# Second layer of a two-layer kernel: scores and the G product as three passes over split operands

## The reference, cut to what matters

```python
x = x + 0.5 * ffn0(layernorm(x))
x = x + attn0(layernorm(x))
x = x + 0.5 * ffn0(layernorm(x))
x = x + 0.5 * experts(layernorm(x))
x = x + attn1(layernorm(x))           # the part that is changed
x = x + 0.5 * experts(layernorm(x))

def attn1(x, Wk, Wq, Wv, Wa, Wb):
    k, q, v = x @ Wk.T, x @ Wq.T, x @ Wv.T
    e = einsum("biq,bjq->bij", q, k @ Wa.T)
    return softmax(e) @ (v @ Wb.T)
```

## Time and profile before

| | us |
|---|---|
| median of 3 runs | 1031.23 (1031.03 to 1032.40) |
| profiled execution, span from first to last instruction | 1028.6 |
| around the span, by the median | 2.6 |
| PE busy in the span | 946.0 (92%) |
| DVE busy | 734.3 (71%) |
| ACT busy | 556.6 (54%) |
| GpSimd busy | 618.5 (60%) |

### The profile page before, as it was taken

The page is one execution under the profiler, slowest core; times in us unless marked ns, Lnnn a source line. Parts: engine busy times, 40 slices in busy tenths (PEclk is TensorE's granted clock), DMA queues, the critical chain, the costliest instruction groups (busy, mean ns, idle before and its releaser), DMA issues. The chain is left out here.

```text
span 1028.6 us, 16112 instructions
## 1 busy us (share of the span) xinstructions
PE 946.0 (92%) x4589; PEld 701.4 (68%) x4589; DVE 734.3 (71%) x2076; ACT 556.6 (54%) x1189; POOL 618.5 (60%) x579
## 2 busy tenths in 40 slices
PE   3999999999999999999999998899988999889994
PEld 2777777777766767767777775488764666658773
DVE  5778789898989889999999976344433667634442
ACT  4554665675857758566555442245425777525441
POOL 4677778777667677676787785434441245433443
PEclk9999999999999999999999999999999999999998
DMA  6880000000000000000000002156524000016561
GB/s 172 354 363 1 1 1 1 1 1 1 1 1 1 1 1 1 1 1 1 11 9 4 11 11 85 54 164 194 174 70 137 1 23 22 22 56 194 174 181 33
DMA packets 42904, 65.17 MB, mean 63 GB/s; under 512 B 7153, under 2 KB 25121, under 8 KB 40640
## 3 DMA queue, kind: packets, MB, share of 16 engines
q1 hardware_dynamic: 37824, 55.59, 16.7%
q0 software_dynamic: 4992, 8.54, 2.6%
HBM read 37.20 MB, written 28.74 MB: 64 GB/s over the span
## 5 line engine op out<-in xcount | busy, mean ns | idle before, releaser
L379 PE MATMUL bank<-split 128*128 128x512 f32 x544 | 245.4, 451 | 9.5 <-DVE ud L1341 3.7
L381 PE MATMUL bank<-split 128*128 128x512 f32 x544 | 216.0, 397 | 0.0
L380 PE MATMUL bank<-split 128*128 128x512 f32 x544 | 214.6, 394 | 0.0
L894 ACT ACTIVATE sil<-bank 128x512 f32<-128x512 f32 x128 | 76.0, 595 | 147.7 <-PE bank L381 147.2
L379 PEld LDWEIGHTS bank<-split 128*128 128x128 f32 x544 | 103.9, 191 | 41.4 <-issue 10.0
L1287 DVE TENSOR_TENSOR act<-act,wT 128x512 f32<-128x512 f32 x128 | 123.1, 962 | 4.4
L380 PEld LDWEIGHTS bank<-split 128*128 128x128 f32 x544 | 104.2, 191 | 26.5 <-issue 10.5
L381 PEld LDWEIGHTS bank<-split 128*128 128x128 f32 x544 | 103.4, 190 | 24.0
L1283 DVE TENSOR_TENSOR act<-bank,sil 128x512 f32<-128x512 f32 x128 | 88.0, 687 | 43.5 <-issue 22.4
L1717 POOL TENSOR_TENSOR act<-act 128x512 f32<-128x512 f32 x64 | 86.6, 1353 | 29.4 <-DVE act L1287 29.2
L1723 POOL TENSOR_TENSOR split<-act,split 128x512 fp32r<-128x512 f32 x64 | 92.5, 1447 | 18.1 <-ACT split L963 17.9
(11 more groups left out here) (294 smaller groups left out, 2011.5 us busy)
## 6 DMA issues: line engine op xcount, KB each, us to landing
e<-e_dram SPq DMA_DIRECT2D x92, 256.0 KB, 3.1
rows_in<-yw SPq DMA_DIRECT2D x17, 1056.0 KB, 18.0
xin<-rows_in SPq DMA_DIRECT2D x46, 132.0 KB, 3.1
x<-rows_out SPq DMA_DIRECT2D x8, 256.0 KB, 5.1
rows_in<-yw,slot_i POOLq DMA_INDIRECT x64, 2.3
rows_out<-ob,ids POOLq DMA_INDIRECT x46, 2.3
out<-ob,ids POOLq DMA_INDIRECT x46, 2.5
act<-b_dram SPq DMA_DIRECT2D x2, 256.0 KB, 3.5
```

The lines of the kernel that those rows point to most:

```text
L379: mm(dst, w[0], m[0], start=start, stop=False, **more)
L380: mm(dst, w[0], m[1], start=False, stop=False, **more)
L381: return mm(dst, w[1], m[0], start=False, stop=stop, **more)
L894: af(sil[(k - 1) % 2][:, :], bank[BH1[STEPS[k - 1][0] % 2]][:, :], ACT.Silu).then_inc(silu_done.sem, 1)
```

## The change

y^T, z^T and G are each kept as two fp32r tiles: a high part, which is the rounded value, and a low part, which is what rounding left off. score and y_G become `mm3` of them. The full-precision yT stays for y_U. zT's fp32 copy is gone; ACT writes the high part in its place. ACT writes y twice (high part, then fp32). DVE makes the low parts of y and z by subtraction (`y_low`, `z_low`), at two new places of its list, and the low part of G once, before the first experts. New waits: TensorE waits for the low parts before score, y_G and y_U, and for G's low part before the first experts; y_low waits for both of ACT's copies of y, z_low for ACT's copy of z. The new tile `yz` holds the parts of y and z.

```diff
-        zT, pr_, pT = mT1, act0[0:2], act0[2:4]
+        pr_, pT = act0[0:2], act0[2:4]
...
+        yz = sb("yz", [P, 8 * S], F32R)
+        yTs = [(yz[:, 4 * i * S:(4 * i + 1) * S], yz[:, (4 * i + 1) * S:(4 * i + 2) * S]) for i in range(2)]
+        zTs = [(yz[:, (4 * i + 2) * S:(4 * i + 3) * S], yz[:, (4 * i + 3) * S:(4 * i + 4) * S]) for i in range(2)]
...
-            sem("yT_saved"), sem("zT_ready"), sem("zT_saved"), sem("v1_ready"), sem("v1_saved"))
+            sem("yT_saved", 2), sem("zT_ready"), sem("zT_saved"), sem("v1_ready"), sem("v1_saved"))
+        yz_low = sem("yz_low", 2)
...
                     pe.wait_ge(*exp_done(main, n - 1))
-                    mm(bank[n % 2][:, :], zT[p][:, rows(n)], yT[p][:, :], start=True, stop=True).then_inc(sc_ready.sem, 1)
+                    pe.wait_ge(*yz_low(main))
+                    mm3(bank[n % 2][:, :], tuple(z_[:, rows(n)] for z_ in zTs[p]), yTs[p], True, True).then_inc(sc_ready.sem, 1)
...
                     pe.wait_ge(*yT_saved(pre))
-                    mm(bank[7][:, :], gmat[:, :], yT[pre % 2][:, :], start=True, stop=True).then_inc(zT_ready.sem, 1)
+                    pe.wait_ge(*yz_low(pre, 1))
+                    mm3(bank[7][:, :], gmats, yTs[pre % 2], True, True).then_inc(zT_ready.sem, 1)
...
                     pe.wait_ge(*zT_saved(pre))
+                    pe.wait_ge(*yz_low(pre))
...
             keep_busy(9)
+            pe.wait_ge(prod_saved.sem, 5)
             tiles(0, 4, expert)
...
-                af(gmat[:, :], bank[2][:, 0:P], ACT.Copy).then_inc(prod_saved.sem, 1)
+                af(gmats[0], bank[2][:, 0:P], ACT.Copy).then_inc(prod_saved.sem, 1)
...
                     act.wait_ge(*ao_ready(pre - 2))
+                    af(yTs[pre % 2][0], bank[7][:, :], ACT.Copy).then_inc(yT_saved.sem, 1)
                     af(yT[pre % 2][:, :], bank[7][:, :], ACT.Copy).then_inc(yT_saved.sem, 1)
...
-                    af(zT[pre % 2][:, :], bank[7][:, :], ACT.Copy).then_inc(zT_saved.sem, 1)
+                    af(zTs[pre % 2][0], bank[7][:, :], ACT.Copy).then_inc(zT_saved.sem, 1)
...
+                def y_low():
...
+                    dve.wait_ge(*yT_saved(pre))
+                    dve.wait_ge(*sc_ready(pre - 2))
+                    v.tensor_tensor(yTs[pre % 2][1], yT[pre % 2][:, :], yTs[pre % 2][0].bitcast(F32), ALU.subtract).then_inc(yz_low.sem, 1)
...
+                def z_low():
...
+                    dve.wait_ge(*zT_saved(pre))
+                    v.tensor_tensor(zTs[pre % 2][1], bank[7][:, :], zTs[pre % 2][0].bitcast(F32), ALU.subtract).then_inc(yz_low.sem, 1)
...
                 maximum(0)
+                y_low()
                 r_stats(r_st, ao_done, -NCH)
                 r_factors(srt)
                 maximum(1)
...
                 r_read(srt, 6)
+                z_low()
                 r_top1(srt)
                 add(0)
                 maximum(3)
...
             dve.wait_ge(prod_saved.sem, 4)
+            v.tensor_tensor(gmats[1], bank[2][:, 0:P], gmats[0].bitcast(F32), ALU.subtract).then_inc(prod_saved.sem, 1)
             tiles(0, 4, expert)
```

More of the change, by code:

```diff
@@ L187, in build @@
         waT = sb("waT", [P, P]); wbT = sb("wbT", [P, P])
-        wak = sb("wak", [P, P]); gmat = sb("gmat", [P, P]); wuT = sb("wuT", [P, P])
+        wak = sb("wak", [P, P]); gmat = sb("gmat", [P, 2 * P], F32R); gmats = gmat[:, 0:P], gmat[:, P:2 * P]; wuT = sb("wuT", [P, P])
         cnt = sb("cnt", [P, E]); cnt_i = sb("cnt_i", [P, E], I32); nt_i = sb("nt_i", [P, E], I32); ntf = sb("ntf", [P, E])
@@ L1648, in y_stats @@
                     aggregate(st, stats_l, part_l, mv_l[st % 2], -0.5, bn_l, stat_l, [(sc_l[st % 2][:, 0, :], *PLAIN)])
+                def y_low():
+                    if pre is None:
+                        return
+                    dve.wait_ge(*yT_saved(pre))
+                    dve.wait_ge(*sc_ready(pre - 2))
+                    v.tensor_tensor(yTs[pre % 2][1], yT[pre % 2][:, :], yTs[pre % 2][0].bitcast(F32), ALU.subtract).then_inc(yz_low.sem, 1)
+                def z_low():
+                    if pre is None:
+                        return
+                    dve.wait_ge(*zT_saved(pre))
+                    v.tensor_tensor(zTs[pre % 2][1], bank[7][:, :], zTs[pre % 2][0].bitcast(F32), ALU.subtract).then_inc(yz_low.sem, 1)
                 maximum(0)
+                y_low()
                 r_stats(r_st, ao_done, -NCH)
```

## The result

The changed kernel takes 1069.24 us (median of four runs, 1066.01 to 1072.36) beside 1031.13 for the kernel before in the same comparison: a ratio of 1.038, 95% interval 1.036 to 1.040. The forecast was 1075, its range 1059 to 1086. The profiled execution took 1067.51, its span 1065.8, against 1028.6 before; the second layer is 40.05 us longer and the rest of the program 2.85 shorter.

The account below looks back on a forecast made before the run. TensorE bounds the second layer now, but the added DVE waits would make DVE's chain late. Span 1028.6 + waits 32.0 + clock falls 11.5 + 2.6 outside the span gave 1075 us, 4.2% slower, range 1059 to 1086.

Parts of the forecast that it names:

- The walk: Second layer's full slot, operation by operation: waits for y_low and z_low lengthen it from 14.15 to 18.78 us, +4.63.
- the fall: TensorE's clock drops in the new pause of about 4 us: 1.6 us a slot, seven slots, 11.5 in all.
- The sum: Whole kernel: profiled span 1028.6 + waits 32.0 + clock 11.5 + 2.6 around the span, 1074.7 us.
- chunk 0's fall: Chunk 0's slot, counted among seven with the new TensorE pause: a clock drop costing 1.6 us.
- The products: score and y_G on TensorE: a split product takes 0.79 us against 0.86, giving back 0.35 us a slot.
- gmat's low part: Before the first experts: making it and TensorE's wait cost nothing, as DVE is idle for 6.42 us there.
- Rival 1: Second layer: waits cost what was forecast, but the clock stays up; 1063 us, chance 22%.
- Rival 2: Second layer: clock falls twice a slot, also in the second pause; another 7 x 1.6, 1086 us, chance 10%.
- Rival 3: Second layer: DVE's waits end before TensorE needs maximum(1), so it stays TensorE-bound; 1024 to 1028 us, chance 3%.

Follow-up runs that it names:

- e1: Changed kernel with y_low moved behind share_of(1) and z_low behind share_of(2) in DVE's list; 1030.69 us, ratio 1.0008 to the kernel before.
- e2: Changed kernel with y_low alone moved later in DVE's list, behind share_of(1); 1047.66 us, ratio 1.017 to the kernel before.
- e3: Changed kernel with z_low alone moved later in DVE's list, behind share_of(2); 1061.44 us, ratio 1.032 to the kernel before.
- e7: Changed kernel with 17 unread products before the second transpose, 2 ahead of r_rank and 6 behind it; 1064.47 us, ratio 1.033 to the kernel before.
- e6: Changed kernel with its copies, subtractions and waits, but score and y_G as single fp32 products; 1073.28 us, ratio 1.041 to the kernel before.
- e8: e1's order, with y_stats first on DVE and unread products (8 and 6) in the slot that only prepares chunk 0; 1028.97 us, ratio 0.9996 to before.
- e9: e8 plus unread products in chunk 0's slot, seven ahead of y_T and four ahead of the first transpose of weights; 1026.51 us, ratio 0.9964 to before.
- e5: Changed kernel without making the low parts of y and z, or waiting for them, from the third chunk on; 1034.49 us, ratio 1.006 to before.
- e4: Changed kernel with 17 unread bf16 products on TensorE ahead of the second transpose of weights; 1068.64 us, ratio 1.038 to the kernel before.

## Why the prediction was right, step by step

**The walk held.** It put maximum(1) at 7.09 us into a full slot (measured 7.02), the second transpose at 8.64 (8.57). From there the clock is low: y_G at 10.13 came at 11.04, z_low at 11.77 at 13.33, maximum(3) at 13.73 at 15.27. The 1.54 us between forecast and measurement at maximum(3) is the fall, which I had put at 1.6 and on exactly this stretch: transpose and mix(0) took 2.47 in place of 1.49, y_G and the hand-over 1.67 in place of 1.00. From maximum(3) to the end of the slot it is 4.95, against 5.05. DVE's idle time ahead of z_low is 4.54 us where I had said 2.5; about 1.6 of it is the fall. e1, e2 and e3 show the mechanism itself, not only its times: move the subtractions behind work that is ready and the loss is gone, move one and a part of it is.

**What the clock is worth** was asked of e7: 1.75 us a full slot, within the 0 to 2.45 that the prediction allowed. So the waits at full clock are 4.32, where the walk had 4.63. That my 1.6 came so close is partly luck. It stood for 3.2 us of work at half speed, as in the first layer; here the clock is low for over 5 us of work, and what counts is the part on the chain: transpose, mix(0), y_G and the hand-over, 4.14 us in place of 2.49. The Trainium skill, "TensorE: Matmul & The Clock Gate", section "Loop structure matters more than you think", shows a long wait (for a DMA, in its example) between matmuls sending the clock down; the trace agrees for a wait on an exponential: 3.69 us of pause, then 0.50.

**The sum came out high.** By the slots, in the order of the prediction (with 1.6 for a fall; seven of them are 11.2, not the 11.5 that stands there):

| | predicted, us | measured, us |
|---|---|---|
| slot that prepares chunk 0, up to y_T of chunk 1 | +3.3 | +3.37 |
| slot of chunk 0 | +2.5 + 1.6 | +2.30 |
| slot of chunk 1 | +3.1 + 1.6 | +4.23 |
| five full slots | +23.2 + 8.0 | +30.38 |
| last slot | -0.1 | -0.23 |
| in the stage | +43.2 | +40.05 |

The stretches end at y_T of chunk 1, at score(0) of chunks 1, 2 and 7, and at the first transpose behind the last mix.

The step that was mis-sized is chunk 0's fall, counted in full. TensorE's clock falls already in the slot ahead, in the pauses for the low parts of y and z, and what follows at half clock lies mostly beside work of ACT and GpSimd. (The walk also had y_U find z_low done. In the full slots it does; in the preparing slot y_U waits 1.50 us for it.) TensorE's rows of the preparing slot and of y_T of chunk 1 in the kernel after, then the clock, and DVE's y_low in chunk 0's slot:

```profile
778.96 0.47 PE L384 MATMUL bank<-yz,gmat 128*128 128x512 f32 x1 [1.99 <-DVE yz L1665]
...
781.39 2.04 PE L796 MATMUL bank<-wuT,tT 128*128 128x128 f32 x8 [1.50 <-DVE yz L1671]
...
786.21 1.12 PE L380 MATMUL bank<-ident,yn_a 128*128 128x128 f32 x4 [1.50 <-ACT yn_a L1221]
```

```profile
780.00:782.00 2.00, 0.61 (x3) 0.53 0.17 60
```

```profile
789.26 0.69 DVE L1665 TENSOR_TENSOR yz<-hT,yz 128x512 fp32r<-128x512 f32 x1 [3.81 <-ACT hT L1201]
```

y_U takes 2.04 us in place of 1.16, but y_T waits for y_norm (`yn_a`), which waits for GpSimd's product of the statistics behind y_low, z_low and y_stats, as the walk had it, and not for the slower y_U. In chunk 0's slot maximum(1), at 789.87, waits for y_low and so for ACT's copy, though TensorE has gone on from score(1) to the next transpose at 788.41, low clock or not. e6, with fp32 products, bears this out: there the clock is back at 1.00 from 786 on, and chunk 0's slot takes 16.27 us all the same, against 16.26. From y_T of chunk 0 to that of chunk 1, before took 6.53 us (777.96 to 784.49) and after 9.90 (776.31 to 786.21).

Outside the stage the kernel after comes out 2.85 us shorter in its profile: its first y_T stands 1.65 earlier, and what follows the last slot is 1.2 shorter. Neither is worked on by the change. The first y_G of e8 and that of e9, with the same work ahead, differ by 0.73 (778.81 and 779.54), so part of it may be spread from one profile to another; its cause stays open. With it the span is 1028.6 + 40.05 - 2.85 = 1065.8, the time around it 1.7 where I had 2.6, and the median of the runs lies 1.7 above the profiled execution.

**The products.** I took 0.35 us a slot, nearest to the first layer's rows; e5 and e1 say 0.43 and 0.5. The step that failed is small: score(3) stands right behind y_G and costs 0.71, not 0.79. The Trainium skill, "FP8 and Floating Point Precision", section "TensorE Precision Notes", gives fp32 four passes; by an estimate from that, three would cost 0.65, and the measured 0.78 and 0.71 don't bear it out.

**gmat's low part** was put at nothing, and the first transposes of the experts start at 663.29 us, beside 663.37 before.

**The rivals.** Rival 1, clock up throughout, did not happen, and e7 shows the waits without the clock's fall. Rival 2, a second fall in each slot, did not happen in the change either, but its place was right: in four of e4's five full slots the clock falls behind the second pause once the first is filled. Rival 3 named the condition for a gain, that the waits end before TensorE needs maximum(1). e1 is that case, made by hand: the slots fall to 13.64, and the slots that prepare and use chunk 0 eat the gain; with these mended (e9) the gain is 0.36%.

## What to carry to other kernels

A step that is put into the list of an in-order engine costs what everything queued behind it waits, not its own duration: the same 1.4 us of subtractions cost 6.6 us a slot in one place and nothing in another. Before moving work off a full engine, walk through one slot and write down when each input is there; then put the new step behind work that is ready. Price the clock with the wait: a new pause on TensorE made what followed run at half speed, and filling it moved most of the loss to the next pause until that was filled too.

## What the runs showed that I had not expected

- Filling the long pause alone gained nothing (e4): in four of five full slots the granted clock then fell behind the next pause of 1.39 us, to 0.58 over the 2 us that follow, though a like pause (1.37) leaves it at 1.00 in the kernel after. What decides this stays open.
- Unread products cost time where there is no pause for them to fill: chunk 0's slot grew from 16.26 to 19.84 in e7.
- A split product gains more at half clock than at full: y_G took 1.43 against 1.70 there, and 0.78 against 0.86 at full clock.
